# Spreading the turned masks over the partitions by transfers through DRAM, in an audio layer with experts

## Chip, cores and metric

The kernel runs on one core of one Trainium2 chip. The metric is the device time of one execution in microseconds (us), the median over several executions.

## What is computed

The reference runs one layer over 8 sequences of 750 rows of 256 numbers. Cut to what matters:

```python
h = tok(x)                          # segments of 256, every 2nd row, softmax attention inside a segment
h = h + attn(layernorm(h))          # circular convolutions and a decaying sum along the sequence
h = h + ffn(layernorm(h))
# ffn, x being the normalised rows:
logits = gelu(x @ router_w1 + b) @ router_w2 + b
topk_p, topk_i = top_k(softmax(logits), 2)          # 2 of 8 experts for each row
for _ in range(2):
    ctx = concat([integrated, v])
    shared_ctrl = gelu(ctx @ shared_w1 + b) @ shared_w2 + b
    for e in range(8):                               # once for each of the row's two choices
        o = gelu(ctx @ expert_w1[e] + b1[e]) @ expert_w2[e] + b2[e]
        out = out + where(idx == e, o, 0)
    # the control vectors drive (x, v); a halting gate mixes old and new
refined = gelu(integrated @ refine_w1 + b) @ refine_w2 + b
out = x + integration_weight * refined
```

## The kernel before

**Tiles and slots.** Every second row of a segment gives a tile of 128 rows; there are 24 tiles (NT), three for each sequence. `run(slot)` calls `slot(t)` for t = -3 to 26 on every engine; each engine's program is this one list, written out by hand, and the engines meet by semaphores (`passed(eng, sem, tile)` waits until a semaphore has counted that tile's events). A slot works on several tiles at once: z = t+3 and e = t+2 (scores and softmax), f = t+1 (attention, normalising, router, first hidden layer), t (first of the two iterations), n = t-1 (second iteration), m = t-2 (its last products), o = t-3 (refining and output). I call "slot t" the slot in which tile t is in its first iteration. Work behind a waiting instruction on the same engine waits too.

**The experts.** All eight experts' hidden units (8 x 64) are computed for all rows, as four chunks of 128 partitions (unit on the partition, row along the free axis): `ge`, after the gelu. A choice j (first or second expert) keeps, for each row, only the units of its expert: `hm = ge * mexp`, where `mexp` holds for each unit and row a 1 or a 0. Hidden values are split into a high and a low part: DVE multiplies the high ones (`mask_hi`, L1040; first chunks 0 and 1, then chunks 2 and 3, then all four for the second choice), GpSimd the low ones (`mask_lo`, L347), and PE multiplies both with the second weights (`expert_hi` L450, `expert_lo` L466).

**The masks.** DVE finds the two experts of each row (L1179 to L1192), and writes `mask` with rows on the partitions. PE turns it (L721) into PSUM, 116 x 256. ACT evicts it twice: the rows that carry the biases to `end` (L949), and the first 8 rows, one for each expert, to `maskT` (L950, 8 x 256 bf16). In the next slot PE multiplies `maskT` with the constant `expandb` (8 x 512 ones and zeros) in four matmuls (L517), which copies each expert's row to its 64 partitions in PSUM, and ACT evicts the result in two halves to `mexp` (L840). `mexp` has three buffers, and is read in two iterations: that of its own slot and, one slot later, the second one.

**The order around it.** On PE, slot t: the halting row (L510), the four matmuls L517, the shared expert (L436, L437), the first refining layer of tile o (`refine_in`, L427 on x2T), the turning of ex (L541), then the experts' matmuls L450. On ACT: `mexp` (L840), `gh` (L816), `eT` (L847) and the evictions of control vectors (L827, L829). On DVE: x1 (L1234), then in the next slot L1040 three times, `gl` (L1054), L1047, h (L1099), xn (L1114). On SP the queue holds the loads of tiles (L299) and the outputs (L324). The input constants come in by large loads at the start (L288).

The waits that matter, as written:

```python
# ACT, slot t
for i, (lo, hi) in enumerate(((0, 4), (4, 8))):
    passed(act, me_ps, t, per=2, step=i + 1)
    AF(mexp[t.s][:, lo:hi, :]..., cd[:, lo * P:hi * P], ACT.Copy).then_inc(me_sb, 1)
# DVE, mask_hi
for i, c in enumerate(PARTS if j == 0 else [slice(0, EC)]):
    passed(dve, me_sb, tile, per=2, step=i + j + 1)
    passed(dve, e_sb, tile, per=2, step=i + j + 1)
    V.tensor_tensor(hm[0][:, j, c, :], ge[:, c, :], pairs(tile, j, c), ALU.mult).then_inc(done, 1)
```

Of the kernel before, what the change touches and what calls it, by code (L numbers as in the profile page):

```python
# [46 lines left out]
           [("expand", EC * P)],  # L47
# [58 lines left out]
def audio_layer(nc, x, params, out):  # L106
# [4 lines left out]
    with ctx:  # L111
# [18 lines left out]
        def staged(name, rows=P):  # L130
# [18 lines left out]
        expandb = sb("expandb", [E, EC, P], bf16)  # L149
# [96 lines left out]
        x_in = [sem(f"x_in{s}") for s in range(NX)]  # L246
        y_out = [sem(f"y_out{s}") for s in range(NS)]
# [4 lines left out]
        (xT_ps, score_ps, eT_ps, att_ps, xnT_ps, retr_ps, xfT_ps, rh_ps, lg_ps, mT_ps, me_ps, s1_ps, e1_ps,  # L252
         halt1_ps, u1_ps, x1T_ps, s2_ps, e2_ps, halt2_ps, u2_ps, x2T_ps, rl1_ps, rl2_ps) = (
            sem(n) for n in ("xT_ps score_ps eT_ps att_ps xnT_ps retr_ps xfT_ps rh_ps lg_ps mT_ps me_ps s1_ps "
                             "e1_ps halt1_ps u1_ps x1T_ps s2_ps e2_ps halt2_ps u2_ps x2T_ps rl1_ps rl2_ps").split())

        (xT_sb, ex_sb, eT_sb, xfT_sb, rh_sb, tw_sb, mT_sb, me_sb, s1_sb, e1_sb, th1_sb, u1_sb, x1T_sb, s2_sb,
         e2_sb, th2_sb, u2_sb, x2T_sb, rg_sb, sp1_sb, sp2_sb, gh1_sb, gh2_sb,
         rgh_sb, eb1_sb, eb2_sb) = (
            sem(n) for n in ("xT_sb ex_sb eT_sb xfT_sb rh_sb tw_sb mT_sb me_sb s1_sb e1_sb th1_sb u1_sb x1T_sb "  # L260
# [23 lines left out]
        def _(sp):  # L284
# [47 lines left out]
        def _(pool):  # L332
# [16 lines left out]
            def slot(t):  # L349
# [59 lines left out]
        def _(pe):  # L409
# [48 lines left out]
            def expert_lo(dst, j, tile, lo_g, end_sb, done, ncols):  # L458
# [8 lines left out]
                passed(pe, end_sb, tile, per=2, step=j + 1)  # L467
# [4 lines left out]
            def expert_control(dst, j, tile, hi_v, end_v, lo_g, end_sb, done, ncols):  # L472
# [4 lines left out]
                expert_lo(dst, j, tile, lo_g, end_sb, done, ncols)  # L477
# [26 lines left out]
            def slot(t):  # L504
                z, f, n, m, o = t.at(3), t.at(1), t.at(-1), t.at(-2), t.at(-3)
                last_in = n.exists() and not t.exists()
                if t.exists():
# [53 lines left out]
                if n.exists():  # L561
# [3 lines left out]
                    elif t.exists():  # L565
                        passed(pe, me_sb, t, per=2)
# [178 lines left out]
        def _(act):  # L745
# [6 lines left out]
            def constants():  # L752
# [558 lines left out]
```

## Time and profile before

| | |
|---|---|
| median of 3 executions | 816.12 us (815.87 to 817.86) |
| the profiled execution | 814.5 us |
| its span, first to last instruction | 812.6 us |
| busy: PE, PE weight loads, DVE, ACT, POOL | 749.5, 650.0, 651.9, 536.0, 274.1 us |
| mean granted clock of PE | 0.966 of full speed |
| HBM read, written | 10.05 MB, 3.15 MB |

Times in the profile count from the span's start. The engines are PE (matrix engine; PEld is its weight loading, which runs beside the matmuls), DVE (vector), ACT (scalar), POOL (GpSimd) and SP (which here only issues transfers). A row names the line of the kernel, the operation, what it writes and reads, and in brackets how long the engine had been idle before and who ended that. Rows of one engine can overlap a little, since instructions are pipelined.

### The profile page before, as it was taken

How to read it: one execution, taken by the hardware profiler on the slowest of the kernel's cores; microseconds unless marked ns; L12 is line 12 of the kernel's file. 1: busy time of each engine (PE TensorE's matmuls, PEld its weight loads, DVE VectorE, ACT ScalarE, POOL GpSimd, SP SyncE). 2: the span in 40 equal slices, each digit the busy share in tenths (PEclk: the TensorE clock that was granted, in tenths of full speed). 3: DMA queues.
4: the chain of work that ended last, by engine and by line, in shares of the span. 5: the costliest groups of instructions: out<-in, count | busy, mean ns of one | idle time of the engine just before them, and what ended most of it. 6: DMA issues, size and time to landing. Idle time of an engine off the chain costs nothing.

```text
span 812.6 us, 14659 instructions
## 1 busy us (share of the span) xinstructions
PE 749.5 (92%) x4784; PEld 650.0 (80%) x4784; DVE 651.9 (80%) x1516; ACT 536.0 (66%) x1334; POOL 274.1 (34%) x393
## 2 busy tenths in 40 slices
PE   4578999999999999999999999999999999999884
PEld 3466888888888888888888888888888888888764
DVE  3447778888889889889889889889889889889652
ACT  1555667677676676676676676685685785775554
POOL 1134333243253252243243243234234334333121
PEclk9577999999999999999999999999999999999997
DMA  8100000000000000000000000000000000000000
GB/s 336 52 8 1 1 1 14 1 15 14 1 14 11 5 14 7 8 15 1 15 13 2 14 14 1 14 14 1 14 14 2 8 8 1 8 8 1 7 8 13
DMA packets 8154, 14.13 MB, mean 17 GB/s; under 512 B 848, under 2 KB 7048, under 8 KB 7568
## 3 DMA queue, kind: packets, MB, share of 16 engines
q1 hardware_dynamic: 8080, 13.20, 4.6%
q8 instruction: 39, 0.64, 0.3%
q14 instruction: 35, 0.29, 0.1%
HBM read 10.05 MB, written 3.15 MB: 16 GB/s over the span
## 4 chain that ended last, share of the span: by engine, by line
PE 46%; DVE 24%; ACT 21%; issue 8%; DMA 1%; POOL 0%; ACTq 0%; POOLq 0%; SPq 0%; DVEq 0%
PE ctl L450 9%; PE ctl L466 7%; PE ctl L427 5%; ACT L776 3%; DVE hm_hi L1040 3%; PE pb L427 3%; ACT ge L809 3%; ACT L787 3%; PE ctl L469 2%; PE pa L427 2%; ACT work L779 2%; DVE both L1208 2%; ACT work L783 2%; PE cd L615 2%; DVE gl L1054 2%
## 5 line engine op out<-in xcount | busy, mean ns | idle before, releaser
L347 POOL TENSOR_TENSOR hm_lo<-gl,mexp 128x256 fp32r<-128x256 f32 x144 | 111.2, 797 | 358.5 <-DVE gl L1054 358.5
L450 PE MATMUL ctl<-w2e_hi,hm_hi 128*128 128x512 f32 (+1 forms) x432 | 160.6, 381 | 10.3 <-DVE hm_hi L1040 10.1
L450 PE MATMUL ctl<-w2e_lo,hm_hi 128*128 128x512 f32 (+1 forms) x432 | 149.6, 360 | 0.0
L827 ACT ACTIVATE work<-ctl 128x256 f32<-128x256 f32 (+1 forms) x144 | 70.6, 490 | 90.3 <-PE ctl L469 90.3
L450 PEld LDWEIGHTS ctl<-w2e_hi,hm_hi 128*128 128x128 f32 x432 | 82.1, 190 | 28.0 <-DVE hm_hi L1040 16.4
L466 PE MATMUL ctl<-w2e_hi,hm_lo 128*128 128x512 f32 (+1 forms) x432 | 102.3, 362 | 0.1
L1040 DVE TENSOR_TENSOR hm_hi<-ge,mexp 128x256 fp32r<-128x256 f32 x144 | 79.4, 579 | 22.3 <-ACT ge L809 16.1
L450 PEld LDWEIGHTS ctl<-w2e_lo,hm_hi 128*128 128x128 f32 x432 | 82.5, 191 | 11.1
L427 PE MATMUL pa<-x1T,par 128*128 128x128 f32 x768 | 89.7, 275 | 0.0
L427 PEld LDWEIGHTS pa<-x1T,par 128*128 128x128 f32 x768 | 87.8, 192 | 0.1
L466 PEld LDWEIGHTS ctl<-w2e_hi,hm_lo 128*128 128x128 f32 x432 | 74.3, 188 | 14.7 <-POOL hm_lo L347 0.8
L809 ACT ACTIVATE ge<-pa,par 128x128 f32<-128x128 f32 x192 | 54.6, 371 | 13.1 <-PE pa L427 13.1
L427 PE MATMUL pa<-xfT,par 128*128 128x128 f32 x384 | 55.8, 291 | 0.0
L829 ACT ACTIVATE work<-ctl 128x256 f32<-128x256 f32 x144 | 55.0, 382 | 0.0
L427 PEld LDWEIGHTS ctl<-x2T,par 128*128 128x128 f32 x384 | 47.9, 197 | 4.3 <-issue 1.3
L427 PEld LDWEIGHTS pa<-xfT,par 128*128 128x128 f32 x384 | 50.1, 203 | 1.1
L427 PE MATMUL ctl<-x2T,par 128*128 128x128 f32 x384 | 48.7, 282 | 1.5 <-issue 1.0
L456 PE MATMUL ctl<-w2a,hm_hi 128*128 128x512 f32 (+1 forms) x144 | 47.8, 386 | 0.0
L800 ACT ACTIVATE sh<-pb,par 128x128 f32<-128x128 f32 x48 | 17.6, 367 | 44.4 <-PE pb L427 44.4
L1070 DVE TENSOR_SCALAR work<-work,w 128x256 f32<-128x256 f32 x72 | 43.3, 655 | 2.9 <-ACT work L829 2.8
L469 PE MATMUL ctl<-w2b,end 128*128 128x512 f32 (+2 forms) x144 | 43.8, 358 | 1.3 <-ACT end L822 1.3
L949 ACT ACTIVATE end<-cd 116x256 fp32r<-116x256 f32 x24 | 9.2, 384 | 52.6 <-PE cd L721 52.6
(167 smaller groups left out, 1733.7 us busy)
## 6 DMA issues: line engine op xcount, KB each, us to landing
work<-params_dram SPq DMA_DIRECT2D x3, 1152.0 KB, 10.3
out_dram<-y SPq DMA_DIRECT2D x24, 128.0 KB, 1.7
xa<-x_dram SPq DMA_DIRECT2D x16, 128.0 KB, 2.7
par<-params_dram SPq DMA_DIRECT2D x1, 1280.0 KB, 12.8
work<-params_dram SPq DMA_DIRECT2D x2, 512.0 KB, 11.1
xa<-x_dram SPq DMA_DIRECT2D x8, 119.0 KB
par<-params_dram SPq DMA_DIRECT2D x1, 512.0 KB, 15.9
par<-params_dram SPq DMA_DIRECT2D x1, 465.0 KB, 4.6
```

The lines of the kernel that those rows point to most:

```text
L347: TT(hm[1][:, j, c, :], gl[:, c, :], pairs(tile, j, c), ALU.mult).then_inc(done, 1)
L427: last = mm(dst[0:rows, c * P:(c + 1) * P], w[:, q, c, :], rhs[:, q, :], start=(q == 0), stop=(q == nk - 1))
L450: mm(dst[:, a:z], hm[0][:, j, c, :], w2e[i][:, c, a:z], start=(c == 0 and i == 0), stop=False)
L456: mm(dst[:, a:z], hm[0][:, j, PC, :], w2a[:, 1 + j, a:z], start=False, stop=False)
L466: mm(dst[:, a:z], hm[1][:, j, c, :], w2e[0][:, c, a:z], start=False, stop=False)
L469: last = mm(dst[:, a:z], end[tile.s][0:rows, j, :], w2b[0:rows, 1 + j, a:z], start=False, stop=True)
L776: nc.scalar.preload_act_table_set("softplus")
L809: last = AF(ge[:, c, :], pa[:, c * P:(c + 1) * P], ACT.Gelu, bias=par[:, a:a + 1])
L827: AF(tan[tile.s][:, 1:kinds, j, :], ctl_t[:, D:kinds * D].rearrange("p (a d) -> p a d", a=kinds - 1), ACT.Tanh, scale=0.5)
L829: AF(rb[tile.s][:, j, :], ctl_t[:, 0:D], ACT.Copy).then_inc(done, 1)
L1040: V.tensor_tensor(hm[0][:, j, c, :], ge[:, c, :], pairs(tile, j, c), ALU.mult).then_inc(done, 1)
L1070: last = V.tensor_scalar(gw[:, j, :], tan[m.s][:, 1, j, :], 1.0, w3[m.s][:, j:j + 1], ALU.add, ALU.mult)
```

## The change

`maskT` is written to a small DRAM tensor, and read back from there eight times, each time one expert's row (512 B, both choices) to 64 partitions of `mexp`. The expansion matrix, its load and its copy, the four matmuls, their two evictions and the semaphores me_ps and me_sb go. The spreading is a new function on SP's queue, last in a slot, behind the slot's output. The readers of `mexp` now wait for two DMA semaphores: me_in[0] counts the first four reads of a tile (chunks 0 and 1), me_in[1] the other four. ACT evicts maskT ahead of end, and `end_sb` marks the second. Waits that stood on me_sb for the sake of PSUM space are taken over by end_sb, x2T_sb and mask_v.

```diff
+        def spread(tile):
+
+            passed(sp, mT_sb, tile)
+            passed(sp, en2_v, tile, back=NS, per=2)
+            passed(sp, hl2_g, tile, back=NS, per=3)
+            sp.dma_start(masks, maskT[:, :, :].rearrange("e j m -> e (j m)")).then_inc(me_out, 16)
+            passed(sp, me_out, tile, per=16)
+            for k in range(E):
+                src = masks[ORDER[k]:ORDER[k] + 1, :].to_broadcast([HID, 2 * P])
+                sp.dma_start(mexp[tile.s][ENDS[k % 2], k - k % 2:k - k % 2 + 2, :].rearrange("p c m -> p (c m)"),
+                             src).then_inc(me_in[k // EC], 16)
...
         def slot(t):
-            z, o = t.at(4), t.at(-3)
+            z, f, o = t.at(4), t.at(1), t.at(-3)
...
+            if f.exists():
+                spread(f)
...
             def mask_lo(tile, j, done, gl_v, read, back):
...
-                passed(pool, me_sb, tile, per=2, step=j + 1)
+                passed(pool, me_in[j], tile, per=16 * EC)
...
-                    passed(pe, mT_sb, t)
-                    if o.exists():
-                        passed(pe, x2T_sb, o)
-                    both = maskT[:, :, :].rearrange("e j m -> e (j m)")
-                    for c in range(EC):
-                        last = mm(cd[:, 2 * c * P:2 * (c + 1) * P], expandb[:, c, :], both, start=True, stop=True)
-                        if c % 2:
-                            last.then_inc(me_ps, 1)
...
                     if t.exists():
-                        passed(pe, me_sb, t, per=2, step=1)
+                        passed(pe, end_sb, t)
...
+                    if o.exists():
+                        passed(pe, x2T_sb, o)
                     nc.tensor.transpose(pc[:, 0:P], ex[:, :], ident).then_inc(eT_ps, 1)
...
-                AF(expandb[:, :, :].rearrange("p c m -> p (c m)"), staged("expand", E), ACT.Copy)
...
-                    for i, (lo, hi) in enumerate(((0, 4), (4, 8))):
-                        passed(act, me_ps, t, per=2, step=i + 1)
-                        AF(mexp[t.s][:, lo:hi, :].rearrange("p c m -> p (c m)"), cd[:, lo * P:hi * P],
-                           ACT.Copy).then_inc(me_sb, 1)
...
                     passed(act, mT_ps, f)
                     passed(act, u2_ps, f, back=NS, per=BR)
-                    AF(end[f.s][0:MR, :, :], pc[0:MR, 0:2 * P].rearrange("p (j m) -> p j m", j=2), ACT.Copy)
+                    for done in me_in:
+                        passed(act, done, f, back=1, per=16 * EC)
                     AF(maskT[:, :, :].rearrange("p j m -> p (j m)"), pc[0:E, 0:2 * P], ACT.Copy).then_inc(mT_sb, 1)
+                    AF(end[f.s][0:MR, :, :], pc[0:MR, 0:2 * P].rearrange("p (j m) -> p j m", j=2),
+                       ACT.Copy).then_inc(end_sb, 1)
...
                 for i, c in enumerate(PARTS if j == 0 else [slice(0, EC)]):
-                    passed(dve, me_sb, tile, per=2, step=i + j + 1)
+                    passed(dve, me_in[i + j], tile, per=16 * EC)
...
+    masks = nc.dram_tensor("masks_dram", (E, 2 * P), _mybir.dt.bfloat16, kind="Internal").ap()
```

The lines of the changed kernel are shifted: L1040 becomes L1038, L450 becomes L463, L427 becomes L440, L541 becomes L547, L299 stays.

How the instructions stand, PE in a slot in the middle of the program, from the halting row to the first expert matmul, before (pb holds the halting row, cd is the PSUM space of masks and turned tiles, ctl that of the control vectors; in brackets the semaphores waited for):

```order
L510 MATMUL pb<-par,sh 128x1 [waits s1_sb]
L517 MATMUL cd<-maskT,expandb 128x256 [waits x2T_sb,mT_sb]
L517 MATMUL cd<-maskT,expandb 128x256 x3
L436 MATMUL ctl<-w2a,sab 128x512 [waits u2_sb,sl1_v]
L437 MATMUL ctl<-w2b,sab 128x512
L427 MATMUL ctl<-x2T,par 128x128 [waits rg_sb,u2_sb,x2T_sb]
L427 MATMUL ctl<-x2T,par 128x128 x7
L541 MATMUL cd<-par,ex 128x128 [waits me_sb,ex_sb]
L450 MATMUL ctl<-w2e_hi,hm_hi 128x512 [waits u2_sb,hm1_v]
```

and after:

```order
L523 MATMUL pb<-par,sh 128x1 [waits s1_sb]
L449 MATMUL ctl<-w2a,sab 128x512 [waits u2_sb,sl1_v]
L450 MATMUL ctl<-w2b,sab 128x512
L440 MATMUL ctl<-x2T,par 128x128 [waits rg_sb,u2_sb,x2T_sb]
L440 MATMUL ctl<-x2T,par 128x128 x7
L547 MATMUL cd<-par,ex 128x128 [waits x2T_sb,end_sb,ex_sb]
L463 MATMUL ctl<-w2e_hi,hm_hi 128x512 [waits u2_sb,hm1_v]
```

The four matmuls are gone, and the turning of ex waits for end_sb and x2T_sb in place of me_sb.

ACT at the end of one slot and the start of the next, before:

```order
L949 ACTIVATE end<-cd 116x256 [waits u2_ps,mT_ps]
L950 ACTIVATE maskT<-cd 8x256
L809 ACTIVATE ge<-pa,par 128x128 [waits e1_ps,gl2_v,hm2_v]
L809 ACTIVATE ge<-pa,par 128x128 x3
L793 ACTIVATE x2T<-cd 128x256 [waits rl1_ps,x2T_ps]
L827 ACTIVATE work<-ctl 128x2x256 [waits u2_ps]
L829 ACTIVATE work<-ctl 128x256
L840 ACTIVATE mexp<-cd 128x512 [waits me_ps,hl2_g,en2_v]
L840 ACTIVATE mexp<-cd 128x512 [waits me_ps]
L816 ACTIVATE gh<-ge 128x512 [waits e1_sb]
```

and after:

```order
L946 ACTIVATE maskT<-cd 8x256 [waits me_in0,me_in1,u2_ps,mT_ps]
L947 ACTIVATE end<-cd 116x256
L811 ACTIVATE ge<-pa,par 128x128 [waits e1_ps,gl2_v,hm2_v]
L811 ACTIVATE ge<-pa,par 128x128 x3
L795 ACTIVATE x2T<-cd 128x256 [waits rl1_ps,x2T_ps]
L829 ACTIVATE work<-ctl 128x2x256 [waits u2_ps]
L831 ACTIVATE work<-ctl 128x256
L818 ACTIVATE gh<-ge 128x512 [waits e1_sb]
```

The two evictions to mexp are gone, maskT stands ahead of end, and gh follows the control vectors directly.

SP's queue in slots of the middle, before:

```order
L324 DMA out_dram<-y 128x256 [waits y_v]
L299 DMA xa<-x_dram 128x256 [waits att_ps]
L324 DMA out_dram<-y 128x256 [waits y_v]
L299 DMA xa<-x_dram 119x256 [waits att_ps]
L324 DMA out_dram<-y 128x256 [waits y_v]
```

and after:

```order
L299 DMA xa<-x_dram 128x256 [waits att_ps]
L335 DMA out_dram<-y 128x256 [waits y_v]
L321 DMA masks_dram<-maskT 8x256 [waits hl2_g,en2_v,mT_sb]
L325 DMA mexp<-masks_dram 64x256 [waits me_out]
L325 DMA mexp<-masks_dram 64x256 x7
L299 DMA xa<-x_dram 119x256 [waits att_ps]
```

Between an output and the next load there are now a write to DRAM, a wait for it, and eight reads.

## Rows read from the trace of the kernel before

**Rows 1.** The page, busy us (share of span), instructions.

```profile
PE 749.5 (92%) x4784; PEld 650.0 (80%) x4784; DVE 651.9 (80%) x1516; ACT 536.0 (66%) x1334; POOL 274.1 (34%) x393
```

**Rows 2.** The chain of waits, in time: start us, length us, what.

```profile
403.69 0.54 PE cd L517 x4
...
412.79 0.33 PE cd L592 x2
...
423.62 0.70 DVE gl L1054
```

**Rows 3.** Timeline of a middle slot: start us, length us, engine, line.

```profile
400.16 0.39 ACT L949 ACTIVATE end<-cd 116x256 fp32r<-116x256 f32 x1 [2.26 <-PE cd L721]
...
400.44 0.36 ACT L950 ACTIVATE maskT<-cd 8x256 bf16<-8x256 f32 x1
...
404.37 1.09 ACT L840 ACTIVATE mexp<-cd 128x512 bf16<-128x512 f32 x2
...
405.63 0.42 DVE L1234 SCALAR_TENSOR_TENSOR x<-vu,xf 128x256 f32<-128x256 f32 x1
...
405.97 0.42 DVE L1040 TENSOR_TENSOR hm_hi<-ge,mexp 128x256 fp32r<-128x256 f32 x1
...
406.31 1.02 DVE L1040 TENSOR_TENSOR hm_hi<-ge,mexp 128x256 fp32r<-128x256 f32 x2
...
406.55 0.48 PE L450 MATMUL ctl<-w2e_hi,hm_hi 128*128 128x512 f32 x1
```

**Rows 4.** DVE's line L1114 (ns min/median/max), and the timeline behind it.

```profile
L1114 DVE TENSOR_SCALAR xn<-h,mv,rs x24: 411/1317/1323, 17.3 to 719.7; 128x256 f32<-128x256 f32 x24
...
412.68 0.20 PEld L592 LDWEIGHTS cd<-par,xn 128*128 128x128 f32 x2 [0.33 <-DVE xn L1114]
```

**Rows 5.** Timeline of ACT at the start.

```profile
23.75 0.61 ACT L756 ACTIVATE expandb<-work 8x512 bf16<-8x512 f32 x1
```

**Rows 6.** The page's outputs (KB, us to landing), and loads by tensor.

```profile
out_dram<-y SPq DMA_DIRECT2D x24, 128.0 KB, 1.7
...
DMA to landing us min/median/max: 2.0/2.7/16.4
```

**Rows 7.** Timeline of SP at the end, and one window (clock, DMA share, GB/s).

```profile
810.48 0.33 SPq L324 DMA_DIRECT2D out_dram<-y  x1
...
811.25:811.85 0.60, 0.00 (x0) 0.00 (x0) 0.00 (x0) 0.00 (x0) 0.00 (x0) 0.50 0.63 219
```

**Rows 8.** SP's timeline: first and last of 13 issues, one small, a steady slot.

```profile
0.74 0.38 SPq L299 DMA_DIRECT2D xa<-x_dram  x1
...
3.49 0.28 SPq L288 DMA_DIRECT2D work<-params_dram  x1
...
6.51 0.74 SPq L288 DMA_DIRECT2D work<-params_dram  x1
...
416.47 0.34 SPq L324 DMA_DIRECT2D out_dram<-y  x1
...
416.85 0.33 SPq L299 DMA_DIRECT2D xa<-x_dram  x1
```

**Rows 9.** Timeline of slots 0, 1, 2: masks evicted, second product.

```profile
37.53 0.38 ACT L949 ACTIVATE end<-cd 116x256 fp32r<-116x256 f32 x1 [0.46 <-PE cd L721]
...
41.49 1.03 DVE L1040 TENSOR_TENSOR hm_hi<-ge,mexp 128x256 fp32r<-128x256 f32 x2
...
60.95 0.38 ACT L949 ACTIVATE end<-cd 116x256 fp32r<-116x256 f32 x1 [2.45 <-PE cd L721]
...
68.48 0.94 DVE L1040 TENSOR_TENSOR hm_hi<-ge,mexp 128x256 fp32r<-128x256 f32 x1
...
93.50 0.38 ACT L949 ACTIVATE end<-cd 116x256 fp32r<-116x256 f32 x1 [2.26 <-PE cd L721]
...
98.10 1.03 DVE L1040 TENSOR_TENSOR hm_hi<-ge,mexp 128x256 fp32r<-128x256 f32 x2
```

More of the change, by code:

```diff
@@ L103, with audio_layer @@
 ENDS = [slice(0, HID), slice(HID, P)]
-def audio_layer(nc, x, params, out):
+def audio_layer(nc, x, params, out, masks):
     fp32, f32r, bf16 = mybir.dt.float32, mybir.dt.float32r, mybir.dt.bfloat16
@@ L246, in audio_layer @@
         x_in = [sem(f"x_in{s}") for s in range(NX)]
+        me_in = [sem(f"me_in{i}") for i in range(2)]
+        me_out = sem("me_out")
         y_out = [sem(f"y_out{s}") for s in range(NS)]
@@ L250, in audio_layer @@
         dve_link = sem("dve_link")
-        (xT_ps, score_ps, eT_ps, att_ps, xnT_ps, retr_ps, xfT_ps, rh_ps, lg_ps, mT_ps, me_ps, s1_ps, e1_ps,
+        (xT_ps, score_ps, eT_ps, att_ps, xnT_ps, retr_ps, xfT_ps, rh_ps, lg_ps, mT_ps, s1_ps, e1_ps,
          halt1_ps, u1_ps, x1T_ps, s2_ps, e2_ps, halt2_ps, u2_ps, x2T_ps, rl1_ps, rl2_ps) = (
-            sem(n) for n in ("xT_ps score_ps eT_ps att_ps xnT_ps retr_ps xfT_ps rh_ps lg_ps mT_ps me_ps s1_ps "
+            sem(n) for n in ("xT_ps score_ps eT_ps att_ps xnT_ps retr_ps xfT_ps rh_ps lg_ps mT_ps s1_ps "
                              "e1_ps halt1_ps u1_ps x1T_ps s2_ps e2_ps halt2_ps u2_ps x2T_ps rl1_ps rl2_ps").split())
-        (xT_sb, ex_sb, eT_sb, xfT_sb, rh_sb, tw_sb, mT_sb, me_sb, s1_sb, e1_sb, th1_sb, u1_sb, x1T_sb, s2_sb,
+        (xT_sb, ex_sb, eT_sb, xfT_sb, rh_sb, tw_sb, mT_sb, end_sb, s1_sb, e1_sb, th1_sb, u1_sb, x1T_sb, s2_sb,
          e2_sb, th2_sb, u2_sb, x2T_sb, rg_sb, sp1_sb, sp2_sb, gh1_sb, gh2_sb,
          rgh_sb, eb1_sb, eb2_sb) = (
-            sem(n) for n in ("xT_sb ex_sb eT_sb xfT_sb rh_sb tw_sb mT_sb me_sb s1_sb e1_sb th1_sb u1_sb x1T_sb "
+            sem(n) for n in ("xT_sb ex_sb eT_sb xfT_sb rh_sb tw_sb mT_sb end_sb s1_sb e1_sb th1_sb u1_sb x1T_sb "
                              "s2_sb e2_sb th2_sb u2_sb x2T_sb rg_sb sp1_sb sp2_sb gh1_sb gh2_sb rgh_sb eb1_sb eb2_sb").split())
@@ L308, in _ @@
             tile_in(Tile(0, 2))
-            staging(1, E)
+            staging(1)
+            staging(4)
+            keeping(2)
             staging(2)
-            staging(5)
-            keeping(2)
+            keeping(3)
             staging(3)
-            keeping(3)
-            staging(4)
+            def spread(tile):
[8 more added lines that the diff above has]
+                                 src).then_inc(me_in[k // EC], 16)
             def slot(t):
-                z, o = t.at(4), t.at(-3)
+                z, f, o = t.at(4), t.at(1), t.at(-3)
                 if z.exists() and z.low > 2:
@@ L456, in expert_end, with expert_lo @@
                     mm(dst[:, a:z], hm[0][:, j, PC, :], w2a[:, 1 + j, a:z], start=False, stop=False)
-            def expert_lo(dst, j, tile, lo_g, end_sb, done, ncols):
+            def expert_lo(dst, j, tile, lo_g, eb_sb, done, ncols):
                 rows = MR if j == 0 else P
@@ L466, in expert_lo @@
                         mm(dst[:, a:z], hm[1][:, j, c, :], w2e[0][:, c, a:z], start=False, stop=False)
-                passed(pe, end_sb, tile, per=2, step=j + 1)
+                passed(pe, eb_sb, tile, per=2, step=j + 1)
                 for a, z in spans(ncols):
@@ L470, in expert_lo, with expert_control @@
                 last.then_inc(done, 1)
-            def expert_control(dst, j, tile, hi_v, end_v, lo_g, end_sb, done, ncols):
+            def expert_control(dst, j, tile, hi_v, end_v, lo_g, eb_sb, done, ncols):
                 for a, z in spans(ncols):
@@ L476, in expert_control @@
                 expert_end(dst, j, tile, end_v, ncols)
-                expert_lo(dst, j, tile, lo_g, end_sb, done, ncols)
+                expert_lo(dst, j, tile, lo_g, eb_sb, done, ncols)
             def refine_in(o):
@@ L555, in slot @@
                     if t.exists():
-                        passed(pe, me_sb, t, per=2)
+                        passed(pe, mask_v, t)
                     else:
@@ L1244, in _pack @@
     a["ident"][:] = np.eye(P)
-    for k, e in enumerate(ORDER):
-        a["expand"][e, k * HID:(k + 1) * HID] = 1
     raised = np.zeros((P, 3), np.float32)
@@ L1307 @@
     out = nc.dram_tensor("out_dram", (NT * P, D), _mybir.dt.float32, kind="ExternalOutput").ap()
-    audio_layer(nc, *args, out)
+    masks = nc.dram_tensor("masks_dram", (E, 2 * P), _mybir.dt.bfloat16, kind="Internal").ap()
+    audio_layer(nc, *args, out, masks)
     r = _run(nc, [arrays], core_ids=[0])
```

15 lines of the change are left out of this document (4 added, 11 removed).

## The prediction

> **What bounds the kernel now.** I read the page's busy shares first: PE is busy 92% of the span and DVE 80% [rows 1], so it looks like a PE kernel, and the change takes work off PE. Then the chain of waits, in order of time, for one slot in the middle of the run (a slot is one step of the pipeline, 30.9 us, and 21 of them, tiles 3 to 23, are alike). The chain lies on PE through the four removed matmuls (0.54 us of it at 403.69) to L592 at 412.79 and a few us on, then on ACT, and from 423.62 on DVE until the next x2 [rows 2]. So the removed matmuls stand on the printed chain. The question is whether another chain runs beside it with no slack, and the timeline of the same slot answers that.
>
> In it DVE ends x1 (L1234) at 406.05 and goes on at once with the first masked product (L1040, starts 405.97, the rows overlap by DVE's pipelining); PE's first expert matmul L450 starts at 406.55, when that product is there [rows 3]. The expanded mask was ready long before: its two evictions (L840) run from 404.37 to 405.46. So hm_hi is set by DVE's own queue, not by the masks. Further on the normalised tile xn (L1114) comes from that same DVE queue, and PE's weight load for L592 sits idle 0.33 us for it at 412.68 [rows 4]. Both chains meet there: PE arrives at nearly the same moment as DVE. **PE time taken out ahead of 406.5 is therefore worth nothing** unless DVE gets faster too, while **anything that makes DVE start its products later goes into the slot whole**.
>
> **What is removed.** Per tile four matmuls, 0.54 us of PE, covered by DVE's work up to 406.39, as just said: 0 (at most the 0.1 us between the product's end and L450). Two evictions, 1.09 us of ACT: the next ACT step, gh, feeds DVE only after the three products, so 0 as well. At the start ACT's copy of the expansion matrix goes: L756, on the chain before the weight copies, 0.61 us long and 0.52 to its successor's start [rows 5]: -0.5 us once. The small load of that matrix goes too, hidden under the large loads.
>
> **What is added.** One transfer of 8 rows to DRAM, a wait on SP for it, then eight reads, each spreading one row of 512 B over 64 partitions, four on each of two semaphores; the first product needs the first four, the second product and all later ones need all eight. The clock for this starts when ACT may read the turned masks: 400.16 (L949; maskT now goes first, and end, 0.39 us later, is used much later, at L469 of the next slot). From there I count:
>
> - maskT itself 0.36 us (L950 [rows 3]) and about 0.05 to SP: 0.41.
> - The write. The row to go by is the output: 1.7 us from issue to landing for 128 KB [rows 6]. The windows of the last output say how that splits: issued 810.48, all bytes between 811.25 and 811.85 [rows 7], so some 0.5 us of it are bytes. Here there are 4 KB. Bounds 1.3 and 1.7; I take 1.5.
> - SP wakes: 0.05.
> - Seven more issues until the eighth. Bounds: an issue of 8 rows took 0.28 plus 0.04 to the next, 0.32; at the start twelve steps from issue to issue took 0.74 to 6.51, 0.48 each; in a steady slot output and load are 0.38 apart [rows 8]. I take 0.40: 2.8.
> - The last read lands. Loads of 128 KB took at least 2.0 and in the middle 2.7, the latter right behind an output [rows 6]. Here 32 KB come behind other small reads. Bounds 1.6 (2.0 less the bytes) and 2.7; I take 1.9.
>
> Sum: 0.41 + 1.5 + 0.05 + 2.8 + 1.9 = 6.66 us after 400.16. The fourth read is there at 5.06. DVE starts the first product at +5.81 (covered by 0.75) and the second at 406.31, that is +6.15 [rows 3]: **late by 0.51 us**. With all lower bounds the sum is 5.6 (covered), with all upper ones 8.2 (late by 2.1).
>
> Behind that wait stands all of DVE's queue: third product, gl, the small products, h, xn; so xn is late by 0.5, and with it L592, and then ACT's table loads and the next slot's DVE work. The distance from the masks to the products does not grow with the slot, because DVE is busy without a gap between them. 21 x 0.51 = 10.7 us.
>
> Two early slots differ. In slot 0 the second product starts at 41.49, only 3.96 after 37.53, and in slot 2 at 98.10, 4.60 after 93.50 [rows 9]: late by 2.7 and 2.1. In them xn takes 0.41 and not the usual 1.32 (shortest and median of L1114 [rows 4]), so I give each 0.9 in hand: +1.8 and +1.2. Slot 1 starts its second product 7.5 us after the masks (68.48 against 60.95 [rows 9]): 0.
>
> SP's other work: the load of a tile is now queued behind this spreading, but it is issued a whole slot before PE turns it; the output is issued before the wait, and nothing waits for it soon. Both 0. DMA share is near 0 in the middle.
>
> **Sum:** 10.7 + 3.0 - 0.5 = +13.2. Against the profiled execution's 814.5 that is 827.7; the median of the three runs is 816.1, 1.6 above the profiled one, so about **829**.
>
> At one place a rule speaks against the form of the change. SP issues eight times, 2.8 us by the rows above, which is more than the lateness. The Trainium skill, "DMA: Bandwidth & Descriptors", section Rules for kernel authors, says of many small transfers to coalesce them into one, since under 64 KB one pays mostly overhead. By it the same bytes in one read would be ready at 3.9 and the steady slots would lose nothing; the trace before shows no such small read either way.
>
> **Rivals.**
> *Covered.* The short terms hold (issue near 0.32, landing near 1.6), the eighth read is there by 6.15, and the steady slots stay at 30.9. For it: the 8-row issue of 0.28 and the idle DMA engines. Against: eight reads of one freshly written 4 KB stretch, which no row shows. Slots 0 and 2 still lose 1.3 and 0.65: +1.4, 817.6.
> *Full latencies.* The output's 1.7 and the load's median 2.7 hold for small transfers too: 7.66, late by 1.51. 21 x 1.51 = 31.7, early slots 2.8 + 2.2, less 0.5: +36, 852. The Trainium skill, "DMA: Bandwidth & Descriptors", section Anatomy of one DMA, gives a fixed cost of about 2.0 us per transfer, mostly the write receipt (for transfers issued by GpSimd); with 2.0 for both, an estimate from that page, the sum would be 7.3 and the time about 843. The trace's output of 1.7 in all for 128 KB lies below it.
> *Faster.* PE's queue, not DVE's, decides at 412.7, and the transfers are covered. Then the 0.54 us at 403.69 come out of each steady slot: 21 x 0.54 = 11.3, less the 1.4 of the start: 806. It decides from the point where DVE's first product is ready before PE has done with refine; the rows show PE only 0.1 behind it, and the idle weight load at L592 speaks against.
>
> **How the numbers follow.** Forecast (late by 0.1 to 1.2, 819 to 843) 0.42; covered 0.31; full latencies or more 0.19; faster 0.08. The range leaves out faster and the upper part of full latencies: 815 to 852; the forecast's own is 819 to 843. A change of 0.3% (2.4 us) is about the least that a measurement of this kernel can tell. Covered falls nearly all inside it, with a sliver of the forecast: same 0.30, faster 0.08, slower 0.62.
>
> **What would show it.** The slot length (output to output on SP) 31.4 instead of 30.9; on SP eight issues about 0.40 apart, beginning some 2 us after maskT; a wait of DVE's L1040 (now L1038) for the DMA, about 0.5 us 21 times, on the second product and not on the first; more idle before xn's reader on PE. If DVE waits for the first product, the write or the landing was mis-sized; if the waits are there but the slot stays at 30.9, the claim that DVE has no slack is wrong; if there are no DMA waits and the slot is shorter, PE was the bound.

## The result, and the profile after

| | before | changed |
|---|---|---|
| median, 4 executions each on one chip | 816.0 us | 875.49 us (873.41 to 876.9) |
| span of the profiled execution | 812.6 us | 871.6 us |
| mean granted clock of PE | 0.966 | 0.964 |
| output to output on SP, steady slot | 30.9 us | 33.2 us |
| HBM read | 10.05 MB | 16.33 MB |

The ratio is 1.0728, with a 95% interval of 1.0694 to 1.0763: slower by 59.5 us. The direction was forecast; 829 us was not, and the range's upper end of 852 lies 23 us below the result.

The page of the changed kernel: busy time of each engine, the chain that ended last by engine, and the reads of the masks (number, KB each, us from issue to landing).

```profile
PE 753.9 (86%) x4688; PEld 642.0 (74%) x4688; DVE 653.9 (75%) x1516; ACT 515.3 (59%) x1285; POOL 274.0 (31%) x393
...
PE 36%; ACT 18%; DVE 15%; SPq 11%; DMA 10%; issue 8%; POOL 2%; DVEq 0%; ACTq 0%; POOLq 0%
...
mexp<-masks_dram SPq DMA_DIRECT2D x192, 32.0 KB, 2.5
```

Against [rows 1], PE has 96 instructions fewer (its busy time is 4 us longer all the same, which was not followed up) and ACT 49 fewer and 21 us less, and the span is 59 us longer. SP's queue and the DMA transfers now hold 21% of the chain.

The waits of the changed kernel: who waited for what, us in total, times, the longest.

```profile
DVE hm_hi L1038 <- DMA mexp<-masks_dram: 60.0, 30, 5.9
...
PE ctl L463 <- DVE hm_hi L1038: 49.5, 51, 5.2
...
PEld cd L596 <- DVE xn L1112: 23.2, 21, 3.1
```

DVE waits 60.0 us for the masks, and PE behind it. A middle slot on the timeline, to be laid beside [rows 3]:

```profile
431.52 0.37 ACT L946 ACTIVATE maskT<-cd 8x256 bf16<-8x256 f32 x1 [2.26 <-PE cd L725]
...
431.92 0.28 SPq L321 DMA_DIRECT2D masks_dram<-maskT  x1
...
433.14 4.93 SPq L325 DMA_DIRECT2D mexp<-masks_dram  x8
...
437.00 0.43 DVE L1232 SCALAR_TENSOR_TENSOR x<-vu,xf 128x256 f32<-128x256 f32 x1
...
437.51 0.42 DVE L1038 TENSOR_TENSOR hm_hi<-ge,mexp 128x256 fp32r<-128x256 f32 x1
...
438.12 0.58 SPq L299 DMA_DIRECT2D xa<-x_dram  x1
...
440.02 1.03 DVE L1038 TENSOR_TENSOR hm_hi<-ge,mexp 128x256 fp32r<-128x256 f32 x2 [2.09 <-DMA mexp<-masks_dram]
...
440.51 0.50 PE L463 MATMUL ctl<-w2e_hi,hm_hi 128*128 128x512 f32 x1 [1.32 <-DVE hm_hi L1038]
```

x1 starts 5.48 us after the masks may be read (437.00 against 431.52), as before (5.47). The first product starts at +5.99 where it was at +5.81; its row names no wait, but it is 0.18 later than before. The second starts at +8.50 where it was at +6.15: **late by 2.35 us**, and the steady slots grew by 2.34 (means of 18 slots, 33.22 and 30.88). The chain of waits, from 431 on, has the terms of my sum one by one:

```profile
431.52 0.38 ACT maskT L946
431.92 1.20 DMA masks_dram<-maskT
433.14 0.45 SPq L325
433.63 0.60 SPq L325
...
436.83 0.60 SPq L325
437.48 2.52 DMA mexp<-masks_dram
440.02 0.06 DVE hm_hi L1038
```

| term | forecast (bounds) | measured |
|---|---|---|
| maskT to the issue of its write | 0.41 | 0.40 |
| the write, issue to landing | 1.5 (1.3 to 1.7) | 1.20 |
| SP wakes | 0.05 | 0.02 |
| seven more issues | 2.8 (0.32 to 0.48 each) | 4.34 (0.49, then 0.64 each) |
| last read, issue to landing | 1.9 (1.6 to 2.7) | 2.52 |
| DVE starts | 0 | 0.02 |
| sum, against 6.15 | 6.66: late 0.51 | 8.50: late 2.35 |

Then 21 slots x 2.34 = 49.1 us. The rest, 9.9 us, is lost before the masks of tile 3 are there (they may be read from 122.31 before, and from 132.17 now). Slots 0 and 2 of the changed kernel, for [rows 9]:

```profile
36.70 0.37 ACT L946 ACTIVATE maskT<-cd 8x256 bf16<-8x256 f32 x1 [0.46 <-PE cd L725]
...
42.66 0.42 DVE L1038 TENSOR_TENSOR hm_hi<-ge,mexp 128x256 fp32r<-128x256 f32 x1 [5.94 <-DMA mexp<-masks_dram]
...
45.22 1.03 DVE L1038 TENSOR_TENSOR hm_hi<-ge,mexp 128x256 fp32r<-128x256 f32 x2 [2.13 <-DMA mexp<-masks_dram]
...
96.67 0.37 ACT L946 ACTIVATE maskT<-cd 8x256 bf16<-8x256 f32 x1 [2.26 <-PE cd L725]
...
105.13 1.03 DVE L1038 TENSOR_TENSOR hm_hi<-ge,mexp 128x256 fp32r<-128x256 f32 x2 [2.07 <-DMA mexp<-masks_dram]
```

The second product is at +8.5 in both, where it was at +3.96 and +4.60: late by 4.6 and 3.9, and here even the first product waits. The 9.9 us come apart into three pieces: the masks of tile 0 are there 0.8 us earlier (36.70 against 37.53), slots 0 and 1 together lose 4.0, and slot 2 loses 6.7. In slot 2 this is more than its lateness. The windows of this kernel behind that wait (us of the window and its length; busy us and count of PE, PEld, DVE, ACT, POOL; granted clock; DMA share; GB/s):

```profile
100.00:120.00 20.00, 16.61 (x90) 13.76 (x88) 11.52 (x27) 10.31 (x24) 5.92 (x10) 0.83 0.07 20
120.00:140.00 20.00, 17.61 (x103) 14.76 (x101) 13.70 (x37) 11.16 (x35) 3.95 (x5) 0.91 0.05 14
```

In the kernel before the granted clock of PE was 1.00 in both. PE's weight loads had sat idle for the products for 3.33 us until 103.11 and for 1.14 until 105.61, and what follows ran at the lower of its two levels (1.2 instead of 2.4 GHz) from 103 to 109 (0.50 granted) and in part from 121 to 127 (0.84, then 0.60); from tile 2's masks to tile 3's took 28.8 us before and 35.5 after. By these windows of 3 us the lower level took away at most some 4.9 us of full-speed time, an estimate (6 x 0.50, and 3 x 0.06, 0.16 and 0.40 for those from 109, 121 and 124); 2.8 us were lost beyond the lateness.

### The profile page after: what moved, and what is told of

Same layout as the page of the kernel before. It is cut to its first block, busy times and chain, and to the rows that moved or that the text cites. A ratio compares the mean times of both kernels' runs of the same rounds, so it can differ in the third digit from the quotient of the medians.

```text
span 871.6 us, 14635 instructions
## 1 busy us (share of the span) xinstructions
PE 753.9 (86%) x4688; PEld 642.0 (74%) x4688; DVE 653.9 (75%) x1516; ACT 515.3 (59%) x1285; POOL 274.0 (31%) x393
## 3 DMA queue, kind: packets, MB, share of 16 engines
HBM read 16.33 MB, written 3.24 MB: 22 GB/s over the span
## 4 chain that ended last, share of the span: by engine, by line
PE 36%; ACT 18%; DVE 15%; SPq 11%; DMA 10%; issue 8%; POOL 2%; DVEq 0%; ACTq 0%; POOLq 0%
PE ctl L463 13%; SPq L325 11%; DMA mexp<-masks_dram 7%; PE pb L440 4%; PE pa L440 3%; PE ctl L479 3%; ACT L778 3%; DMA masks_dram<-maskT 3%; DVE xn L1112 3%; ACT L789 3%; DVE hm_hi L1038 2%; ACT work L781 2%; ACT work L785 2%; PE cd L619 2%; PE ctl L508 2%
## 5 line engine op out<-in xcount | busy, mean ns | idle before, releaser
L463 PE MATMUL ctl<-w2e_hi,hm_hi 128*128 128x512 f32 (+1 forms) x432 | 165.8, 393 | 49.8 <-DVE hm_hi L1038 49.5
L463 PE MATMUL ctl<-w2e_lo,hm_hi 128*128 128x512 f32 (+1 forms) x432 | 151.6, 364 | 0.0
L463 PEld LDWEIGHTS ctl<-w2e_hi,hm_hi 128*128 128x128 f32 x432 | 83.2, 193 | 80.4 <-DVE hm_hi L1038 68.4
L1038 DVE TENSOR_TENSOR hm_hi<-ge,mexp 128x256 fp32r<-128x256 f32 x144 | 81.0, 577 | 79.1 <-DMA mexp<-masks_dram 60.0
L463 PEld LDWEIGHTS ctl<-w2e_lo,hm_hi 128*128 128x128 f32 x432 | 83.9, 194 | 10.3
L440 PE MATMUL pa<-x1T,par 128*128 128x128 f32 x768 | 89.7, 275 | 0.0
L440 PEld LDWEIGHTS pa<-x1T,par 128*128 128x128 f32 x768 | 87.8, 192 | 0.1
L440 PEld LDWEIGHTS ctl<-x2T,par 128*128 128x128 f32 x384 | 46.3, 197 | 17.3 <-issue 16.6
L440 PE MATMUL ctl<-x2T,par 128*128 128x128 f32 x384 | 50.0, 285 | 8.1 <-issue 7.3
L440 PE MATMUL pa<-xfT,par 128*128 128x128 f32 x384 | 55.2, 289 | 0.0
L802 ACT ACTIVATE sh<-pb,par 128x128 f32<-128x128 f32 x48 | 17.6, 367 | 59.5 <-PE pb L440 59.5
L440 PEld LDWEIGHTS pa<-xfT,par 128*128 128x128 f32 x384 | 49.7, 202 | 1.1
L384 POOL TENSOR_TENSOR rg_lo<-rg,rg_hi 128x512 fp32r<-128x512 f32 x24 | 30.8, 1284 | 35.8 <-ACT rg_hi L774 35.8
```

What stands on the lines that cost most here:

```text
L440: last = mm(dst[0:rows, c * P:(c + 1) * P], w[:, q, c, :], rhs[:, q, :], start=(q == 0), stop=(q == nk - 1))
L463: mm(dst[:, a:z], hm[0][:, j, c, :], w2e[i][:, c, a:z], start=(c == 0 and i == 0), stop=False)
```

## The experiments

The theory: (a) DVE's queue sets the slot and the lateness of the second product goes in whole; (b) the lateness comes from eight issues in a row; (c) what the change takes off PE and ACT is worth nothing. The rivals: the reads are slow to land however few they are; or PE was the bound and gained its 0.54 us a slot, which the waits hide. Ratios are to the kernel before, run on the same chip; intervals are 95%.

**Two reads in place of eight.** With the experts in another order, each half of the partitions is one read of 2 KB to 64 partitions. This order changes the last chunk's pair, so that some rows' choices fall on other experts; the instructions and their sizes stay.

```diff
-ORDER = [1, 2, 3, 4, 5, 6, 0, 7]
+ORDER = [0, 4, 1, 5, 2, 6, 3, 7]
...
-                for k in range(E):
-                    src = masks[ORDER[k]:ORDER[k] + 1, :].to_broadcast([HID, 2 * P])
-                    sp.dma_start(mexp[tile.s][ENDS[k % 2], k - k % 2:k - k % 2 + 2, :].rearrange("p c m -> p (c m)"),
-                                 src).then_inc(me_in[k // EC], 16)
+                rows = masks.rearrange("(i c) m -> i (c m)", i=2)
+                for i in range(2):
+                    src = rows[i:i + 1, :].to_broadcast([HID, 2 * EC * P])
+                    sp.dma_start(mexp[tile.s][ENDS[i], :, :].rearrange("p c m -> p (c m)"), src).then_inc(me_in, 16)
```

> The changed kernel with its eight reads of 64 rows x 512 B put into two of 64 rows x 2 KB (the experts' order in the weights is changed so that each half of the partitions reads one stretch of DRAM). Theory A (the loss is the lateness of the transfers, and the lateness is mostly eight issues of 0.62 us in a row): the masks are ready 0.40 + 1.22 + 0.6 + 2.5 to 3.0 = 4.7 to 5.2 us after ACT may read the turned masks, before DVE wants them (5.8); no DMA wait before the products from slot 3 on; slot length back to 30.9, and the time 814 to 818. Rival B (bytes or rows of the broadcast set the time, not the number of transfers): 64 KB more per transfer make each four times as long, ready at about 8.5 as in the changed kernel, time 865 to 880. Rival C (PE was the bound, the removed matmuls are worth 0.54 us a slot once the masks are there): 803 to 806.

Measured: 821.88 us, ratio 1.0083 (1.0067 to 1.0099). Its page and its timeline (a steady slot, then slots 0 and 2):

```profile
mexp<-masks_dram SPq DMA_DIRECT2D x48, 128.0 KB, 2.9
```

```profile
437.25 1.09 SPq L326 DMA_DIRECT2D mexp<-masks_dram  x2
...
441.47 1.35 DVE L1037 TENSOR_TENSOR hm_hi<-ge,mexp 128x256 fp32r<-128x256 f32 x3
...
43.11 1.36 DVE L1037 TENSOR_TENSOR hm_hi<-ge,mexp 128x256 fp32r<-128x256 f32 x3 [5.35 <-DMA mexp<-masks_dram]
...
100.67 1.36 DVE L1037 TENSOR_TENSOR hm_hi<-ge,mexp 128x256 fp32r<-128x256 f32 x3 [1.36 <-DMA mexp<-masks_dram]
```

Each read, now four times as large, lands 2.9 us after issue, later than the small reads' 2.5, and yet the steady slots are 30.9 us again without a wait: (b) holds, and some 53 of the 59.5 us went with the six issues fewer. It also shows that lighter PE and ACT queues give nothing at 30.9. The time is 4 us above the upper end that I had expected. What is left is 6.4 us between the last outputs. Of these 4.6 are there at the first output, and the granted clock in the window from 100 to 120 is 0.91. The other 1.8 arise in the last slots and are not the reads': from the 19th output on this kernel takes 117.9 us, the kernel before 116.1, and the next one, without any spreading, 118.0.

**No spreading at all.** The transfers and the waits for them go; `mexp` is set to ones once.

```diff
-                if f.exists():
-                    spread(f)
...
-                passed(pool, me_in[j], tile, per=16 * EC)
...
-                    for done in me_in:
-                        passed(act, done, f, back=1, per=16 * EC)
...
+            for s in range(NS):
+                link(V.memset(mexp[s][:, :, :], 1.0))
...
-                    passed(dve, me_in[i + j], tile, per=16 * EC)
```

> The changed kernel without any spreading: mexp is filled with ones once at the start and never again, nobody waits for it; matmuls, evictions and transfers are all gone (the masking by expert is left out of the result). It tells what the removal alone is worth. Theory A (DVE's queue and PE's meet at the first product with no slack): 813 to 816, slots of 30.9. Rival C (PE or ACT was the bound there): 803 to 806, slots of 30.4.

Measured: 812.79 us, ratio 0.9975 (0.9955 to 0.9994), steady slots 30.9. So (c) holds: with no expansion left anywhere, what is gained is some 2 us in all, and none in the steady slots (the first output is 2.9 us earlier). The rival in which PE was the bound asked for 11 us there.

Where the removed 0.54 us went can be read from ACT's eviction of `ctl` and PE's weight loads for the first refining layer behind it, in the kernel before and in the changed one:

```profile
404.11 0.38 ACT L829 ACTIVATE work<-ctl 128x256 f32<-128x256 f32 x1
...
404.56 1.94 PEld L427 LDWEIGHTS ctl<-x2T,par 128*128 128x128 f32 x16
```

```profile
435.48 0.38 ACT L831 ACTIVATE work<-ctl 128x256 f32<-128x256 f32 x1
...
435.92 1.86 PEld L440 LDWEIGHTS ctl<-x2T,par 128*128 128x128 f32 x16 [0.72 <-issue]
```

Both start +4.40 us after the masks may be read, 0.06 to 0.07 behind the end of the eviction; the layer writes `ctl` and waits for the eviction's semaphore (u2_sb). Without the four matmuls PE stands idle there for 0.72 us. So in the kernel with two reads the first expert matmul comes only 0.08 us earlier (+6.31 against +6.39), and these 0.08 us turn up as more idle time before xn's reader (0.41 in place of 0.33). Most of the removed time never reached the point where DVE covers PE.

**A probe of the transfers.** The kernel before, with added loads of the input to an unused tensor in each slot, for which no engine but SP waits: eight shapes in turn.

```diff
+                kind = tile.n % 8
+                rows = [64, 64, 128, 128, 32, 16, 64, 128][kind]
+                cols = [128, 128, 128, 128, 128, 128, 512, 256][kind]
+                for i in range(1024 // cols):
+                    if kind in (1, 2, 7):
+                        src = x[0:rows, 0:cols]
+                    elif kind == 6:
+                        src = two[i:i + 1, :].to_broadcast([rows, cols])
+                    else:
+                        src = x[i:i + 1, 0:cols].to_broadcast([rows, cols])
+                    sp.dma_start(scr[0:rows, i * cols:(i + 1) * cols], src).then_inc(probed, 16)
```

> The kernel before, with its matmuls and evictions, plus transfers into a spare buffer at the place where the change has its reads, for which nobody waits but SP. The shapes change from tile to tile (eight kinds in turn): 64 rows x 512 B from one row and from 64 rows, 128 rows x 512 B from 128 rows and from one, 32 and 16 rows x 512 B from one, 64 rows x 2 KB from one, 128 rows x 1 KB from 128. Theory A (transfers cost only by being waited for): 815 to 818. Rival D (they hurt by traffic or by SP's queue): 830 or more. From issue to issue: if the zero step of the source makes it slow, 0.62 with one source row and 0.4 with 64; if rows are paid for, 64, 32 and 16 rows take 0.62, 0.3, 0.2 and 128 rows 1.2; if each transfer has a fixed price when the queue is not empty, all take about 0.6, that of 2 KB rows too.

Measured: 815.14 us, ratio 1.0009 (0.9992 to 1.0025). SP's timeline, first issue to the end of the last, in the order 64 rows from one source row, 128 from 128, 128 from one, 32 from one, 16 from one (all 512 B a row), 64 of 2 KB from one, 64 from 64:

```profile
274.95 4.95 SPq L337 DMA_DIRECT2D scr<-x_dram  x8
...
336.70 3.66 SPq L337 DMA_DIRECT2D scr<-x_dram  x8
...
367.60 3.65 SPq L337 DMA_DIRECT2D scr<-x_dram  x8
398.39 3.58 SPq L337 DMA_DIRECT2D scr<-x_dram  x8
429.30 3.57 SPq L337 DMA_DIRECT2D scr<-x_dram  x8
460.19 1.11 SPq L337 DMA_DIRECT2D scr<-x_dram  x2
...
552.81 4.95 SPq L337 DMA_DIRECT2D scr<-x_dram  x8
```

**The pace of issues hangs on the rows, and not as I thought:** 0.64 us a step for 64 rows, from one source row or from 64, and 0.46 to 0.47 for 16, 32 and 128. None of the three rules that I had set down beforehand fits. (In two of the 24 slots one issue alone took 1.14 and 1.71 us; the slots shown have none such.) Neither the freshly written source nor the spreading of one row makes the issue slow. The landings (min/median/max) for 128 rows from 128 source rows, from one source row, and 64 from one:

```profile
DMA to landing us min/median/max: 1.8/1.9/2.1
...
DMA to landing us min/median/max: 2.5/2.7/3.2
...
DMA to landing us min/median/max: 2.4/2.5/2.9
```

Sharing one source row costs 0.8 us for 128 rows. For 64 it costs 0.4 to 0.5 (2.5 against medians of 2.0 to 2.1 from 64 rows in the three slots), and 2.5 is what the masks' reads took too.

**GpSimd's operation moved, in the kernel before.** In a steady slot xn takes 1.3 us beside GpSimd's `rg_lo`; here `rg_lo` stands behind hx. This tests (a) from the other side: if DVE's queue sets the slot, a faster xn shortens it as far as PE's arrival lets it.

```diff
-                if o.exists():
-                    passed(pool, rgh_sb, o)
-                    passed(pool, rl2_ps, o, back=1)
-                    TT(rgp[1][:, :, :], rg[:, :, :], rgp[0][:, :, :].bitcast(fp32), ALU.subtract).then_inc(rgl_g, 1)
                 if f.exists():
...
                     TT(hx[:, :], h[:, :], xn[:, :], ALU.add).then_inc(hx_g, 1)
+                if o.exists():
+                    passed(pool, rgh_sb, o)
+                    passed(pool, rl2_ps, o, back=1)
+                    TT(rgp[1][:, :, :], rg[:, :, :], rgp[0][:, :, :].bitcast(fp32), ALU.subtract).then_inc(rgl_g, 1)
```

> The kernel before with one step moved: on GpSimd the low part of the refining units (rg_lo, 1.29 us) comes behind hx and not ahead of it, so that DVE's xn does not run beside it. Theory A (PE and DVE arrive together at the turning of xn): xn takes 0.41 and not 1.31, DVE comes 0.9 earlier there, but PE does not; gain of 0 to 0.1 us a slot, time 813 to 817. Rival E (DVE alone is the bound): 0.9 x 21, 797.

Measured: 812.15 us, ratio 0.9961 (0.9947 to 0.9975), slots of 30.64. Its DVE line (ns min/median/max) and timeline, against [rows 4]:

```profile
L1114 DVE TENSOR_SCALAR xn<-h,mv,rs x24: 412/414/416, 17.9 to 715.6; 128x256 f32<-128x256 f32 x24
```

```profile
410.45 0.37 PEld L592 LDWEIGHTS cd<-par,xn 128*128 128x128 f32 x2
```

xn is down by 0.9 us, the idle time of 0.33 before L592 is gone, and the slot is shorter by 0.23 (means of 15 slots, 30.87 and 30.64). Both chains did meet there, though DVE came 0.2 to 0.3 us later than PE and not 0 to 0.1 as I had written; the time is 1 us below the lower end that I had expected.

**Three reads.** An order of the experts that keeps the last chunk's pair and needs three reads, of four, three and one of the experts' rows.

```diff
+ORDER = [1, 4, 2, 5, 3, 6, 0, 7]
...
+                flat = masks.rearrange("e m -> (e m)").unsqueeze(0)
+                for done, half, chunk, row, n in ((0, 1, 0, 4, 4), (0, 0, 0, 1, 3), (1, 0, 3, 0, 1)):
+                    src = flat[:, row * 2 * P:(row + n) * 2 * P].to_broadcast([HID, n * 2 * P])
+                    sp.dma_start(mexp[tile.s][ENDS[half], 2 * chunk:2 * (chunk + n), :].rearrange("p c m -> p (c m)"),
+                                 src).then_inc(me_in[done], 16)
```

> The changed kernel with three reads in place of eight (half B's four rows, half A's first three, and A's last row), possible since expert 0 can only be a row's first choice and expert 7 only its second, so that the other six may be put in another order. Ready 0.4 + 1.2 + 0.6 + 2.9 = 5.1 us after the turned masks for the first product (wanted at 5.8), about 5.3 for the second (6.15). If the lateness of the reads is the whole loss: no DMA wait from slot 3 on, slots of 30.9, two early slots late by about 1 to 2 us each, 815 to 822, as with two reads. If the removed 0.54 us of PE were worth something: slots of 30.4.

Measured: 822.3 us, ratio 1.0084 (1.0061 to 1.0106), slots of 30.9, like two reads.

**Five reads.** The order of the change is kept; two reads for the first two chunks, three for the others.

```diff
+                for half, src in ((0, pairs_of[1:2, 0:2, :]), (1, pairs_of[0:1, 1:3, :])):
+                    sp.dma_start(mexp[tile.s][ENDS[half], 0:4, :].rearrange("p (c j) m -> p c (j m)", j=2),
+                                 src.to_broadcast([HID, 2, 2 * P])).then_inc(me_in[0], 16)
...
+                for half, chunk, row, n in ((0, 2, 5, 1), (0, 3, 0, 1), (1, 2, 6, 2)):
```

> The changed kernel, its experts in the old order, with five reads in place of eight (two rows each where two rows belong to the same half and lie evenly spaced). A dose between three and eight. Ready 0.4 + 1.2 + four issues of 0.62 + 2.6 = 6.7 for the second product, wanted at 6.15: late by 0.5, slots of 31.4, 826 to 834. If the loss were not by lateness but by the traffic of the reads (same bytes), 870 to 880 as with eight.

Measured: 838.02 us, ratio 1.0273 (1.0236 to 1.031), slots of 31.6. Waits and timeline of this kernel:

```profile
DVE hm_hi L1044 <- DMA mexp<-masks_dram: 23.4, 25, 5.0
```

```profile
444.76 1.25 SPq L326 DMA_DIRECT2D mexp<-masks_dram  x2
...
450.00 1.03 DVE L1044 TENSOR_TENSOR hm_hi<-ge,mexp 128x256 fp32r<-128x256 f32 x2 [0.62 <-DMA mexp<-masks_dram]
```

Of eight, five and three reads the slots are 33.2, 31.6 and 30.9: three fewer take off 1.6 us, some 0.5 each, and from then on DVE's own work covers the spreading. For five reads I had expected 31.4 and 826 to 834. maskT started at 443.14 in that slot, so the second product is at +6.86, late by 0.71, and the slot grew by 0.7: again whole.

**Can the freed PE time be used?** In the three-read kernel GpSimd's `rg_lo` is moved as above (three_pool); the shared expert, the refining layer and the first expert matmuls are put behind the turning of ex, with ex's product ahead of them (three_early); or both (three_early_pool). The second edit, on PE:

```diff
-                    shared_control(ctl[0], sab1, u1_ps, 2 * D)
-
-                if o.exists() and not last_in:
-                    refine_in(o)
...
+                    shared_control(ctl[0], sab1, u1_ps, 2 * D)
+
+                if o.exists() and not last_in:
+                    refine_in(o)
...
+                if t.exists():
+                    passed(pe, hm1_v, t, per=3, step=1)
...
+                    expert_hi(ctl[1], 0, t, hm1_v, 0, 2 * D)
```

> Three reads, and rg_lo on GpSimd moved behind hx. In the kernel before this move made slots of 30.64 from 30.9. If PE and DVE share the bound behind the first product, the relief of PE ahead of it adds nothing: slots of 30.6 again, 811 to 817. If the relief of PE can be used once DVE is faster: slots of 30.1, 803 to 806.

> Three reads and the three PE steps moved ahead of the experts' matmuls, with rg_lo at its old place on GpSimd. It completes the square with three reads alone (slots of 30.89), with rg_lo moved (30.60) and with both (30.55). If DVE's xn, which runs beside rg_lo for 1.31 us, binds at the turning of xn, the steps on PE are worth nothing without the other move: slots of 30.9, 817 to 823. If PE alone binds: slots of 30.6 or less, 812 or below.

> Three reads, rg_lo moved, and on PE three steps ahead of the experts' first matmuls, into the time that the removed matmuls left: the turning of ex before the shared expert, the attention matmuls and the turning of x1 after the refining layer (0.87 us of work, of which 0.54 fit into the hole). Only possible with the four matmuls gone, since they used the same PSUM. Theory A (PE's stretch from the first product to the turning of xn is what binds; only work taken out of it helps): slots of 30.1 to 30.3, 800 to 808. Rival: DVE or ACT binds as well and the slots stay at 30.6, 811 to 817.

| kernel | us | ratio (interval) | steady slot |
|---|---|---|---|
| three_reads | 822.3 | 1.0084 (1.0061 to 1.0106) | 30.9 |
| three_early | 818.36 | 1.0033 (1.0017 to 1.0049) | 30.9 |
| three_pool | 815.34 | 0.9989 (0.9969 to 1.0009) | 30.60 |
| three_early_pool | 810.32 | 0.9937 (0.9915 to 0.996) | 30.55 |

Three_pool answers half of the question already: with xn early, its slots are 30.60 where before_pool's are 30.64, so that even then the freed PE time is worth 0.05 us and not the 0.5 of the rival. In a steady slot PE's order is worth nothing by itself, since xn still comes late; the timeline of three_early shows PE waiting for it:

```profile
443.00 1.31 DVE L1115 TENSOR_SCALAR xn<-h,mv,rs 128x256 f32<-128x256 f32 x1 [0.65 <-POOL rs L381]
...
444.36 0.20 PEld L599 LDWEIGHTS cd<-par,xn 128*128 128x128 f32 x2 [0.51 <-DVE xn L1115]
```

Its gain of 4 us over three_reads is early: the first output comes at 139.37 in place of 144.43. In slot 2 DVE waits about as long for the masks (1.21 against 1.36 us), but PE has work in the meantime (its weight loads sit idle for 1.33 and not for 2.38 us), the granted clock stays at 1.00 from 100 to 140 (0.90 and 0.93 in three_reads), and from tile 2's masks to tile 3's takes 29.0 us and not 32.9. That is the nearest that these runs come to showing what the clock cost in slot 2; the moved work and the clock are not told apart.

With both edits xn is early and PE no longer waits for it, but before the refining layer PE's weight loads stand idle for 0.66 us. The timeline of three_early_pool:

```profile
433.40 1.86 PEld L442 LDWEIGHTS ctl<-x2T,par 128*128 128x128 f32 x16 [0.66 <-issue]
...
440.19 0.42 DVE L1115 TENSOR_SCALAR xn<-h,mv,rs 128x256 f32<-128x256 f32 x1 [0.65 <-POOL rs L381]
...
441.08 0.38 PEld L599 LDWEIGHTS cd<-par,xn 128*128 128x128 f32 x2
```

It is the wait on `ctl` that was shown above; the 0.54 us taken off PE mostly became waiting at that point, and I got slots of 30.55 and 810.32 us where I had expected 30.1 to 30.3 and 800 to 808. That ACT's eviction ends this wait is read from the layer's semaphore and from the times (+4.4 us in every steady slot looked at); the profile names no releaser, and I made no run that moves the eviction. Still three_early_pool is the only version of the new spreading that beats the kernel before, by 0.6% (before_pool's ratio is 0.9961, on another chip; the intervals overlap, and the two aren't ranked).

## Why the prediction was wrong in size and right in direction

- *Where the chains meet.* Right: xn's idle time before L592 goes when xn is faster, and slots without any masks are 30.9. Only the slack was off, 0.23 us instead of 0 to 0.1.
- *The removed matmuls and evictions worth 0.* Right in value, by the kernel without spreading, and for a reason that was only half mine. I had the 0.54 us covered by DVE's work up to 406.39; the rows show most of it lost before, where PE waits for ACT to empty `ctl`, and only 0.08 us reaching the place where DVE covers it. The printed chain, which ran through the removed matmuls [rows 2], would have promised 11 us.
- *Lateness goes in whole, on the second product and not on the first.* Right: late 2.35, slot +2.34. The first product is not quite clear of it: the fourth read landed at about +5.9, and it started at +5.99 in place of +5.81.
- *The write, 1.5 us.* Too long by 0.3, and below my lower bound. *SP wakes, 0.05*: right.
- **The step that failed: "Seven more issues until the eighth ... I take 0.40: 2.8."** They took 4.34, so +1.54 of the 1.84 us that were missing. My bounds of 0.32 and 0.48 came from transfers of 8 and 128 rows [rows 8] and I took a length between them for granted at 64 rows; the probe puts 64 rows outside that pair, at 0.64. The trace before had rows to widen the bound with, which I left out: the load of 119 rows took SP 0.94 us at 385.95 and 1.31 at 478.54, where that of 128 took 0.33. An upper bound of 0.94 would have reached the result. With all the upper bounds that I did write the sum was 8.2, and by it the time would have been about 865; my range ended at 852 and the run at 875.
- *"The last read lands ... I take 1.9."* It took 2.52, inside its bounds: +0.62, of which the probe gives 0.4 to 0.5 to the shared source row.
- *Early slots +3.0, start -0.5.* Together they cost 9.9 and not 2.5. The lateness there was 4.6 and 3.9 us instead of 2.7 and 2.1, as follows from the same wrong sum; but the granted clock behind the waits was no term at all. Two reads, with a wait of 1.36 us in slot 2, still lose 4.6 us by the first output. Whether the start gained the 0.5 us stays open: the masks of tile 0 came at 37.53 before, and at 36.70, 37.73 and 37.53 with eight, two and five reads.
- *The whole miss.* 21 x 1.84 us in the steady slots are 38.6, the early part 7.4: 46 of the 46.5 us between 829 and 875.5.
- *The rule cited against the change.* The Trainium skill, "DMA: Bandwidth & Descriptors", section Rules for kernel authors, says to coalesce many small transfers into one large one. The two-read kernel agrees: its steady slots are 30.9. My own figure beside it, 3.9 us until one read would be ready, was short: two reads took 5.38 and 5.03 in slots 0 and 2. The Trainium skill, "DMA: Bandwidth & Descriptors", section Anatomy of one DMA, gives about 2.0 us fixed for each transfer issued by GpSimd. Here SP issues, and the trace has 1.20 for the write and 2.52 for the last read: near in sum (3.72 against 4.0) and not one by one. The estimate of 843 that I made with it fell short for the same reason as mine, the issues.
- *The rivals.* "Full latencies" had the right size of landing and too fast an issue; "covered" is what two or three reads show; "faster" fell.

## What to carry to other kernels

When one engine issues many small transfers in a row, price the row of issues first: here it was 4.34 us of 8.50, and landing times mattered less. Bound the price of an issue by every issue row in the trace, also the odd long ones, and not only by those with fewer and more rows than yours. (Sharing the issues out over two engines' queues was not tried.) And before work is taken off the engine with the highest busy share, look for the waits of that engine on others in the same slot, all of them and not only the first that explains it: here PE was held first by ACT's eviction and then by DVE's xn, and what was removed was worth nothing, while a wait put into DVE's queue counted in full.

## What the runs showed of the hardware that I had not expected

- Issues of 64-row transfers on SP follow each other every 0.64 us, those of 16, 32 and 128 rows every 0.46 to 0.47; why 64 rows are slower than 128 was not tried. The load of a tile behind the eight reads took SP 0.58 us (438.12), behind an output 0.33 (416.85 [rows 8]).
- A transfer that reads the same 512 B row for all partitions lands later than one from separate rows: 2.7 against 1.9 us for 128 rows, 2.5 against 2.0 to 2.1 for 64.
- The 8-row write to DRAM landed in 1.20 us, the 128 KB output in 1.7 [rows 6].
- PE's granted clock was 0.83 and 0.91 in the two windows behind a wait of some microseconds in slot 2 (1.00 in the kernel before), and the stretch from tile 2's masks to tile 3's grew by 6.7 us where the lateness in it was 3.9.
- DVE's xn takes 1.31 us while GpSimd's `rg_lo` runs and 0.41 without it; moving the latter by one place was worth 0.23 us a steady slot, and no edit on PE alone was worth anything there.
